# Grouping the value products of two steps into one block of a fused attention kernel

## What is computed

```python
h = layernorm(x) * (1 + ca) + sa
q = (h @ Wq.T)                    # 8 heads of 64
kv = h @ Wkv_down.T               # rank 64
k, v = kv @ Wk_up.T, kv @ Wv_up.T # 8 heads of 64
attn = softmax(q k^T / 8)
x = x + ga * ((attn v) @ Wo.T)
h = layernorm(x) * (1 + cb) + sb
x = x + gb * (h @ weight.T + pooled(h) @ disha)
```

## Time and profile before

| | |
|---|---|
| median of 3 runs | 3649.52 us (3647.22 to 3652.0) |
| profiled execution | 3651.17 us, span of the core 3649.2 us |
| mean granted TensorE clock | 0.983 of full speed |
| TensorE matmul busy | 3530.1 us, 97% |
| GpSimd busy | 2515.4 us, 69% |
| VectorE busy | 2446.3 us, 67% |
| ScalarE busy | 1684.6 us, 46% |

### The profile page before, as it was taken

One profiled execution on the slowest core, in us unless ns is written; L12 is line 12 of the kernel. 1 busy time (PEld: TensorE's weight loads), 2 busy tenths in 40 slices (PEclk: granted clock), 3 DMA queues, 4 the chain that ended last, 5 costly groups with the idle time before them and its releaser, 6 DMA issues.

```text
span 3649.2 us, 50991 instructions
## 1 busy us (share of the span) xinstructions
PE 3530.1 (97%) x15014; PEld 1840.0 (50%) x15014; DVE 2446.3 (67%) x2846; ACT 1684.6 (46%) x3075; POOL 2515.4 (69%) x1513
## 2 busy tenths in 40 slices
PE   5999999999999999999999999999999999999997
PEld 3444555545454554545545455454555545555454
DVE  4667667676676767657676576766767667676663
ACT  1445445444454545445454354543545445454443
POOL 1677767676776767668677676866767677686775
PEclk7999999999999999999999999999999999999998
DMA  1101010010101001010010100101010010100101
GB/s 55 35 20 48 24 56 21 30 48 27 47 26 55 18 27 53 24 51 18 33 47 24 51 27 27 50 27 48 21 41 36 27 48 27 53 18 33 35 30 32
DMA packets 98076, 129.24 MB, mean 35 GB/s; under 512 B 11120, under 2 KB 62448, under 8 KB 97776
## 3 DMA queue, kind: packets, MB, share of 16 engines
q1 hardware_dynamic: 97776, 125.64, 9.9%
HBM read 41.11 MB, written 16.81 MB: 16 GB/s over the span
## 4 chain that ended last, share of the span: by engine, by line
PE 94%; DVE 3%; issue 2%; ACT 1%; POOL 0%; DMA 0%; SPq 0%; DVEq 0%; POOLq 0%; ACTq 0%
PE ps_mix L543 28%; PE ps_max L593 18%; PE ps_score L564 14%; PE ps_score L566 13%; PE ps_side_b L531 7%; PE ps_side_b L651 5%; PE ps_side_a L638 4%; PE ps_side_b L669 3%; PE ps_side_a L631 1%; PE ps_side_a L658 1%; DVE h_lo L972 1%; PE ps_side_a L608 0%; DVE recip L931 0%; DVE neg_max L950 0%; PE ps_side_a L622 0%
## 5 line engine op out<-in xcount | busy, mean ns | idle before, releaser
L811 POOL TENSOR_TENSOR prob_sum<-prob_sum,probs 128x1024 f32<-128x1024 f32 x768 | 1837.5, 2393 | 575.7 <-ACT probs L710 518.7
L950 DVE TENSOR_REDUCE neg_max<-ps_max 128x1 f32<-128x1024 f32 x1016 | 1243.5, 1224 | 721.1 <-PE ps_max L593 710.9
L710 ACT ACTIVATE probs<-ps_score 128x512 f32<-128x512 f32 x2048 | 1113.0, 596 | 1140.9 <-PE ps_score L566 1129.2
L543 PE MATMUL ps_mix<-probs,values 128*64 128x512 f32 x4096 | 1109.5, 620 | 0.0
L564 PE MATMUL ps_score<-query,key_hi 128*128 128x512 f32 x2048 | 839.8, 410 | 37.2 <-issue 35.8
L566 PE MATMUL ps_score<-query_m,key_lo 128*128 128x512 f32 x2048 | 810.2, 396 | 0.0
L593 PE MATMUL ps_max<-key_hi,query 128*128 128x512 f32 x2032 | 749.8, 450 | 5.1 <-DVE neg_max L950 5.0
L593 PEld LDWEIGHTS ps_max<-key_hi,query 128*128 128x128 f32 x2032 | 304.5, 189 | 830.4 <-issue 433.6
L811 POOL TENSOR_TENSOR prob_sum<-probs 128x1024 f32<-128x1024 f32 x128 | 305.5, 2387 | 457.7 <-ACT probs L710 457.7
L931 DVE RECIPROCAL recip<-recip 128x128 f32<-128x128 f32 x512 | 481.4, 942 | 17.8 <-ACT recip L761 17.8
L564 PEld LDWEIGHTS ps_score<-query,key_hi 128*128 128x128 f32 x2048 | 387.5, 189 | 155.2 <-issue 73.9
(11 more groups left out here) (115 smaller groups left out, 2701.8 us busy)
## 6 DMA issues: line engine op xcount, KB each, us to landing
query_m<-query SPq DMA_DIRECT2D x128, 512.0 KB, 3.2
x_in<-in_L_attn_x_dram SPq DMA_DIRECT2D x16, 1024.0 KB, 5.5
x_mid<-in_L_attn_x_dram SPq DMA_DIRECT2D x64, 256.0 KB, 6.9
out_dram<-x_mid SPq DMA_DIRECT2D x64, 256.0 KB, 2.2
h_t<-gates_scratch SPq DMA_DIRECT2D x16, 256.0 KB, 6.7
query_m<-max_row SPq DMA_DIRECT2D x128, 4.0 KB
mixed<-in_L_wmod_dram SPq DMA_DIRECT2D x1, 1536.0 KB, 11.3
mixed<-in_L_attn_Wq_dram SPq DMA_DIRECT2D x1, 512.0 KB, 4.9
```

The source lines that it names most:

```text
L543: last = nc.tensor.matmul(ps_mix[g % 2][j * R:j * R + R, :], values[par][:, k, :], probs[:, s % RING, j * HALF:(j + 1) * HALF], start=(k = ...
L710: nc.scalar.activation(probs[:, s % RING, half * HALF:(half + 1) * HALF], ps_score[half], ACT.Exp, scale=SCALE).then_inc(exps_done, 1)
L811: nc.gpsimd.tensor_tensor(out=total[:, :], in0=before, in1=probs[:, s % RING, :], op=ALU.add).then_inc(adds_done, 1)
L950: nc.vector.tensor_reduce(neg_max[:, m:m + 1], z.max_bank(m, ps_max, ps_scores)[:, :], AX_X, ALU.max, negate=True).then_inc(maxima_done, 1)
```

## The change

`slot` on TensorE is cut into functions, and their order changes. In even steps: scores, then the mixes of the two steps before in one block, then the denominators, then the maximum, then the rest of the side work. In odd steps: scores, maximum, side work. The last two steps of a batch are mixed in step 0 of the next slot. The `max_row` product becomes a transposition. The other engines' lists are unchanged.

```diff
+MIXED = 2
...
+            def mixes(z, s):
+                if s == 0 and z.has_o:
+                    if not z.has_c:
+                        need(pe, exps_done, 2 * STEPS * z.c)
+                    zo = Slot(z.o, 1 - z.par)
+                    for t in range(STEPS - MIXED, STEPS):
+                        mix(zo, t)
+                if s > 0 and z.has_c and s % MIXED == 0:
+                    if s == MIXED:
+                        need(pe, a_drained, values_drained(z))
+                    for t in range(s - MIXED, s):
+                        mix(z, t)
...
             def slot(z):
                 for s in range(STEPS):
...
-                    if s == 0 and z.has_o:
-                        if not z.has_c:
-                            need(pe, exps_done, 2 * STEPS * z.c)
-                        zo = Slot(z.o, 1 - z.par)
-                        mix(zo, STEPS - 1)
-                    if s > 0 and z.has_c:
-                        if s == 1:
-                            need(pe, a_drained, values_drained(z))
-                        mix(z, s - 1)
...
+                    scores(z, s)
+                    if s % MIXED == 0:
+                        mixes(z, s)
+                        side_work(z, s, denominators=True)
+                    maximum(z, s)
+                    side_work(z, s, denominators=False)
...
                         elif kind == "max_row":
...
-                            last = nc.tensor.matmul(side[0:NT, 0:P], neg_max[:, NT * i:NT * (i + 1)], ident[:, :],
-                                                    start=True, stop=True)
+                        last = nc.tensor.transpose(side[0:NT, 0:P], neg_max[:, NT * i:NT * (i + 1)], ident[:, :])
```

More of the change, by code:

```diff
@@ L547, in mix, with scores @@
                     last.then_inc(group_done, 1)
+            def scores(z, s):
+                g, k = divmod(s, NT)
+                if z.has_c:
+                    if k == 0:
+                        need(pe, max_row_set, 16 * (GROUPS * z.c + g + 1))
+                    if s == 0:
+                        need(pe, key_row_set, 16 * (z.c + 1))
+                        if isinstance(z.c, int) and z.c == 0:
+                            pe.wait_ge(maxima_done, STEPS - MAX_LAG)
+                    for j in range(2):
+                        need(pe, exps_done, 2 * (STEPS * z.c + s) - 1 + j)
+                        nc.tensor.matmul(ps_score[j], key_hi[z.par][:, k * P:(k + 1) * P],
+                                         group_queries(g)[:, j, :], start=True, stop=False)
+                        nc.tensor.matmul(ps_score[j], key_lo[z.par][:, k * P:(k + 1) * P],
+                                         query_m[:, g % 2, j * HALF:(j + 1) * HALF],
+                                         start=False, stop=True).then_inc(scores_ready, 1)
@@ new lines, in maximum @@
+            def maximum(z, s):
+                item = z.max_item(s)
+                if item:
+                    b, m = item
+                    gm, unit = divmod(m, NT)
+                    hm, qt = 2 * (gm // 2) + unit // 4, 4 * (gm % 2) + unit % 4
+                    kpar = (1 - z.par) if s >= MAX_LAG else z.par
+                    if m % (2 * NT) == 0:
+                        made = ("query", gm + 1)
+                        here = made in [p[2:4] for p in z.lists[1] if (p[4] == 0) == (s < MAX_LAG)]
+                        need(pe, b_drained, z.through(1, *made) + 1 if here else z.before(1))
+                    need(pe, maxima_done, STEPS * b + m - (0 if z.has_c else 1))
+                    bank = z.max_bank(m, ps_max, ps_scores)
+                    for half in range(2):
+                        last = nc.tensor.matmul(bank[:, half * HALF:(half + 1) * HALF],
+                                                query[:, hm, qt * P:(qt + 1) * P],
+                                                key_hi[kpar][:, half * HALF:(half + 1) * HALF],
+                                                start=True, stop=True)
+                    last.then_inc(max_scores_ready, 1)
@@ L549, in slot @@
             def slot(z):
                 for s in range(STEPS):
[L551 to L568, removed]
@@ L569, in slot @@
-                    if s == 0 and z.has_o:
-                        if not z.has_c:
-                            need(pe, exps_done, 2 * STEPS * z.c)
-                        zo = Slot(z.o, 1 - z.par)
-                        mix(zo, STEPS - 1)
-                    if s > 0 and z.has_c:
-                        if s == 1:
-                            need(pe, a_drained, values_drained(z))
-                        mix(z, s - 1)
[L579 to L595, removed]
-                                                    start=True, stop=True)
-                        last.then_inc(max_scores_ready, 1)
@@ L598, in slot @@
[L598 to L630, removed]
-                            last = nc.tensor.matmul(side[0:NT, 0:P], neg_max[:, NT * i:NT * (i + 1)], ident[:, :],
[L632 to L663, removed]
-                            need(pe, b_drained, count)
-                            products = [(hp, wp, f) for f in range(NF)
-                                        for hp, wp in ((h2_hi, w_ffn_hi), (h2_lo, w_ffn_hi), (h2_hi, w_ffn_lo))]
-                            for j in range(CT):
-                                for q, (hp, wp, f) in enumerate(products):
-                                    last = nc.tensor.matmul(side[:, j * D:(j + 1) * D], hp[:, f, j * P:(j + 1) * P],
-                                                            wp[:, f, :], start=(q == 0), stop=(q == len(products) - 1))
-                        last.then_inc(full[bank], 1)
```

72 lines of the change are left out of this document (added).

## The result

The changed kernel takes 3656.47 us (median of 20 runs, 3655.08 to 3661.39), the kernel before 3648.93 us in the same job (20 runs, 3645.25 to 3652.0). The ratio is 1.0022, 95% interval 1.0015 to 1.0029: slower, by 7.5 us. The forecast had 3670, slower by 20.5. The direction and the main places of the loss are as forecast; the size is less than half of it.

A forecast was written before the change was run, and what follows sets the result against it. TensorE, busy 97%, was taken to bound the kernel; its 244 us saving would be eaten by uncovered waits, leaving +1.1 us a batch, +21 on 3651.2: 3672, or 3670 as a median, range 3622 to 3725.

The forecast's parts named there:

- the scores' wait in the `norm2_t` pairs: Four pairs per batch: even scores wait while ScalarE drains until m + 2.23, m the first max matmul; +0.27 us each.
- the gain of the `ffn` pairs: Four pairs per batch: ffn covers the maximum, out_proj the scores in three; 3 x -0.36, once -0.25, together -1.33 us.
- The gain on TensorE: Fewer form changes: 0.36 us saved per pair of steps and per denominator; with the transposition 244 us taken alone.
- The rival with the block's inside at 0.48: Inner mix pairs of a block take 0.48 us, not 0.43: +64 us, 3734; chance 0.14.
- Maximum even to maximum odd: Odd maximum starts 2.04 us behind the even one; TensorE waits 0.54 for VectorE's reduction plus 0.11 weight load: 0.65.
- Bare pairs: Step pairs (even, odd) without side work in the even step: 5.51 us against 5.22, +0.29 each, 1.45 per batch.
- The rival without waits: TensorE's saving stays and no waits arise, by the mode-change rule: 3406 us; chance 0.06.
- cheap restarts: Waits come but weights load during them, so 0.11 falls away at about 26 waits a batch: -46, 3624 us; chance 0.14.
- Scores odd to scores even: Even scores wait for ScalarE's exponentials: just enough time if ScalarE is free, not enough if it first drains side work.
- The sum: All pairs +1.1 us per batch; fourteen full batches +16, first batch +3.7 more, last about +1: together +21 us.
- Pairs 14 and 16: Pair 14: latent chain unchanged, maximum 0.86 us later, +0.86. Pair 16: the 0.65 wait and latent behind h_lo, +0.5.
- Edits at nothing: GpSimd's adds, earlier denominators, VectorE's later odd reduction and the DMA queue's waits were put at no cost.

The follow-up runs named there:

- a_den_behind: The changed kernel with the denominators back behind the maximum, as a block of their own: 3696.95 us, 1.0131 of the kernel before.
- after: The changed kernel itself, compared with the kernel before: 3656.47 us, ratio 1.0022.
- mix_first2: Changed kernel with mixes, denominators and maximum ahead of scores in even steps, and queries, mixed_lo and ffn moved later: 3653.97 us, 1.0014 of the kernel before.
- a_product: The changed kernel with the old float32 product for max_row in place of the transposition: 3674.56 us, 1.0073 of the kernel before.

## Why the prediction was right in sign and too large in size

The mechanism held: cheaper blocks on TensorE, and two waits that the mix had covered. Two terms of the sum were mis-sized and fail, the scores' wait in the `norm2_t` pairs (+0.12 measured, +0.27 forecast) and the gain of the `ffn` pairs (−1.9 us a batch measured, −1.33 forecast). In a sum whose terms cancel to +1.1 us a batch, these two decide the size.

*The gain on TensorE*: right. 0.86 for the second mix of a block (0.43 twice), 0.36 for the denominators, by the chain and by `a_den_behind`. The rival with the block's inside at 0.48 falls. The transposition was put between a quarter of 0.44 and 0.52; it takes the lower end, 0.11 with no restart. In after that changes nothing in a pair, as the forecast said, because the maximum waits there anyway.

*Maximum even to maximum odd*: right in kind and size. The two maxima start 2.04 apart, and in after the wait is seen (83.0 us); half a reduction removes it and 114 us. Bare pairs +0.30 for +0.29, `max_row` −0.19 for −0.23. The rival without waits falls. So does "cheap restarts" as the forecast posed it, since bare pairs cost what they do with the 0.11 in them.

*Scores odd to scores even*: right in kind, and too large for `norm2_t`, a failed term: +0.12 for +0.27, 0.6 us a batch. I had let ScalarE drain `h_t` for the 1.02 of its row from m + 1.21, until m + 2.23, and only then start the exponentials. In after:

```profile
1955.22 0.73 PE L587 MATMUL ps_max<-key_hi,query 128*128 128x512 f32 x2
...
1956.42 1.02 ACT L789 ACTIVATE h_t<-ps_side_a,mod 128x256 f32<-128x256 f32 x2 [2.34 <-PE ps_side_a L656]
...
1957.34 1.08 ACT L732 ACTIVATE probs<-ps_score 128x512 f32<-128x512 f32 x2
...
1957.99 0.50 PE L565 MATMUL ps_score<-query,key_hi 128*128 128x512 f32 x1
```

The exponentials start at m + 2.12, 0.92 behind the start of a record of 1.02: neighbouring records of ScalarE overlap by 0.1. The scores resume at m + 2.77, and with the 0.10 that this first matmul takes longer at m + 2.87, against 3.03. About 0.11 of the 0.16 is this overlap, and 0.03 stands in the forecast's 3.03 beyond its own 2.85 + 0.04 + 0.11; the rest is not placed. The query pairs are off by less (+0.08 for +0.12), and not by this: there the scores start 2.32 behind the last query matmul (1916.62 to 1918.94), where the forecast had 2.30.

*`ffn`*: the other failed term, −1.9 us a batch for −1.33. I took the kernel before to be unhindered there ("1.70 covers the maximum"), and it was not: `ffn` stood 0.79 behind its maximum, waiting for the subtraction that GpSimd's add holds. After removes 0.16 of that, because its longer block moves `ffn` back; the rest of the wait stays, since there too `ffn` starts 0.13 behind the end of the subtraction (1961.63 against 1959.77 + 1.73). The groups by line show that the subtraction itself only got longer, before and then after:

```profile
L980 DVE TENSOR_TENSOR h_lo<-h_t,h_hi 128x512 fp32r<-128x512 f32 x64 | 50.6, 791 | 12.0 <-ACT h_hi L694 12.0
```

```profile
L1002 DVE TENSOR_TENSOR h_lo<-h_t,h_hi 128x512 fp32r<-128x512 f32 x64 | 105.6, 1650 | 12.2 <-ACT h_hi L716 12.2
```

*The sum*: in a typical batch all pairs but the last (62) make −0.28 us, where the same terms of the forecast make +0.84. A miss of 1.1 over the 14 full batches is about 16 us. The first batch cost 2.3 (forecast 3.7), the last −0.4 (+1), and the head and the tail, which the forecast left alone, were 1.8 shorter together. On the other side the six loop turns idle 39.0 us for 35.8, +3.2, which the forecast had put at nothing. Of the forecast +21 that leaves about 4, and the profiles differ by 3653.7 − 3649.2 = +4.5. The medians' 7.5 is 3 more, within what single executions of after spread over (6 us). So the errors were partly of opposite sign, and the forecast's total says less than its pairs.

*Pairs 14 and 16*: +0.86 and +0.50, as forecast. *Edits at nothing*: held for TensorE's waits. It waits for an add of GpSimd once, 1.6 us (2.8 in before), and for DMA only in the head. The subtraction `h_lo`, which doubled beside the adds, should not have stood at nothing.

## What to carry to other kernels

Saved form changes count only as far as the engine isn't waiting anyway: when blocks are merged on the bounding engine, list what stood between each pair of dependent steps, and compare it with the answering engine's round trip. Here 2.0 us of reduction had 1.5 us of cover, and merging one step less (`MIXED = 1`) kept the two cheap gains, −72 us. When one engine's order changes, walk the other engines' lists in the same order, since a drain placed behind a late exponential cost more than all that was won. And price the state before with its own waits: a piece that starts 0.79 behind another may need 0.56 of it and wait the rest.

## What the runs showed of the hardware

- A transposition of a 128x8 tile between matmuls of the full array takes 0.11 us and no restart; a float32 product of the same shape takes 0.32 and 0.20 more on the next matmul (−33 us in before).
- VectorE's subtraction of two SBUF inputs (512 columns, 0.68 free) ends 0.54 to 0.55 us behind the GpSimd add that it started beside: it takes 0.75, 1.34 and 1.73 in three kernels and 2.84 in `mix_first2`. In after, `mixed`, which reads PSUM, took its 0.68 with an add running all the while. It works the other way too: an add that starts while such a subtraction runs takes up to 2.73 for 2.38.
- A loop turn idles TensorE 5.4 to 7.6 us in the kernels here, and in `a_product`, which differs from after by `max_row`'s product alone, it idled again for about 2 us right behind it.
- Two ScalarE records that follow each other can overlap by about 0.1, as `h_t` and the exponentials in after, so that a sum of durations overstates a chain. Behind a `query` drain they don't: the exponentials start 0.02 after its end.
